# Value sums of the second attention: from VectorE reductions to accumulating transposes on TensorE

## The reference

```
q = q.reshape(Tq, Bq * H, HD).transpose(1, 0, 2)      # k and v alike
attn = jnp.einsum('nqd,nkd->nqk', q, k) * scale
attn = jax.nn.softmax(attn, axis=-1)                  # over 8 keys
out = jnp.einsum('nqk,nkd->nqd', attn, v)             # the value sums
out = out @ out_w.T + out_b
x = x + attention(xn) + moe(xn)
```

## Time and profile before

| | |
|---|---|
| median of 3 runs | 407.57 us |
| profiled execution, its own time | 408.92 us |
| its span, first to last instruction | 407.1 us |
| mean granted clock of TensorE | 0.937 |
| PE / DVE / POOL / ACT busy | 79% / 85% / 58% / 46% |
| DVE's reductions of prod_pv (L1358) | 32 of 1195 ns, 38.2 us |
| POOL's prod_pv (L783) | 32 of 2212 ns, 69.6 us |

### The profile page before, as it was taken

The page is one execution under the profiler, slowest core; times in us unless marked ns, Lnnn a source line. Parts: engine busy times, 40 slices in busy tenths (PEclk is TensorE's granted clock), DMA queues, the critical chain, the costliest instruction groups (busy, mean ns, idle before and its releaser), DMA issues.

```text
span 407.1 us, 5016 instructions
## 1 busy us (share of the span) xinstructions
PE 323.2 (79%) x1455; PEld 237.0 (58%) x1455; DVE 344.1 (85%) x831; ACT 188.4 (46%) x501; POOL 235.4 (58%) x149
## 2 busy tenths in 40 slices
PE   0267696898898875805129999999999999999995
PEld 0136475777787765704016666666666666666662
DVE  3774997987887964599999899999999999999791
ACT  0535556778678656702122262624426262442521
POOL 9151573553644721095065959778695986867450
PEclk9986998999999999775758999999999999999999
DMA  7620000100100102220000000000000000000000
GB/s 184 209 77 1 2 0 1 54 37 17 52 22 32 53 27 96 91 52 0 1 0 1 2 0 27 2 26 0 0 28 1 26 2 26 1 2 26 0 26 27
DMA packets 13247, 12.49 MB, mean 31 GB/s; under 512 B 1548, under 2 KB 9924, under 8 KB 13220
## 3 DMA queue, kind: packets, MB, share of 16 engines
q1 hardware_dynamic: 10944, 10.10, 7.7%
q0 software_dynamic: 736, 0.95, 1.2%
q10 hardware_dynamic: 1540, 1.12, 0.9%
HBM read 5.88 MB, written 2.10 MB: 20 GB/s over the span
## 4 chain that ended last, share of the span: by engine, by line
PE 54%; DVE 19%; ACT 11%; issue 7%; POOL 6%; DMA 1%; ACTq 1%; POOLq 0%; DVEq 0%
PE Q L833 18%; PE VK L833 16%; PE T L833 9%; PE ND L833 6%; PE T L829 4%; ACT xn L546 4%; POOL prod_qk L773 3%; POOL prod_pv L783 2%; PE Q L829 2%; ACT qkv L503 1%; DMA headmask<-in_c_headsel 1%; ACT Q L585 1%; DVE chosen L1411 1%; DVE bst L1086 1%; DVE scr L1341 1%
## 5 line engine op out<-in xcount | busy, mean ns | idle before, releaser
L783 POOL TENSOR_TENSOR prod_pv<-prob,qkv 128x1024 f32<-128x1024 f32 x32 | 69.6, 2212 | 45.0 <-DVE att L1358 24.3
L686 ACT ACTIVATE sg<-Q 128x512 f32<-128x512 f32 x72 | 43.2, 599 | 97.7 <-PE Q L833 95.0
L773 POOL TENSOR_TENSOR prod_qk<-qkv 128x1024 f32<-128x1024 f32 x32 | 75.9, 2397 | 16.7 <-DVE scr L1341 16.7
L833 PE MATMUL VK<-hid,w 128*128 128x512 f32 x144 | 74.5, 599 | 0.0
L833 PE MATMUL Q<-xT_hi,w_hi 128*128 128x512 f32 x72 | 52.3, 726 | 0.7 <-ACT combT L672 0.7
L1441 DVE TENSOR_TENSOR sgc<-ND,sg 128x512 f32<-128x512 f32 x64 | 43.6, 681 | 6.7 <-PE ND L833 4.7
L1454 DVE TENSOR_TENSOR hid<-T,sgc 128x512 f32<-128x512 f32 x64 | 43.5, 679 | 0.3
L833 PE MATMUL T<-xT_hi,w_hi 128*128 128x512 f32 x72 | 28.9, 401 | 17.0 <-DVE hid L1454 17.0
L833 PE MATMUL Q<-bias,ones 128*128 128x384 f32 (+1 forms) x64 | 32.8, 512 | 9.4 <-ACT qkv L503 5.8
L1341 DVE TENSOR_REDUCE scr<-prod_qk 128x128 f32<-128x1024 f32 x32 | 38.4, 1205 | 0.0
L1358 DVE TENSOR_REDUCE att<-prod_pv 128x128 f32<-128x1024 f32 x32 | 38.2, 1195 | 0.0
(11 more groups left out here) (190 smaller groups left out, 796.9 us busy)
## 6 DMA issues: line engine op xcount, KB each, us to landing
xT_hi<-xTs_hi SPq DMA_DIRECT2D x8, 256.0 KB, 2.3
xT_lo<-xTs_lo SPq DMA_DIRECT2D x8, 256.0 KB, 2.3
out_x<-fin SPq DMA_DIRECT2D x8, 256.0 KB, 2.3
x<-in_x SPq DMA_DIRECT2D x2, 256.0 KB, 4.7
wraw<-in_w1T SPq DMA_DIRECT2D x1, 512.0 KB, 10.8
w<-in_w2T SPq DMA_DIRECT2D x1, 512.0 KB, 4.6
wraw<-in_w3T ACTq DMA_DIRECT2D x1, 512.0 KB, 3.1
sel<-in_c_sel POOLq DMA_DIRECT2D x4, 128.0 KB, 2.8
```

The source lines that it names most:

```text
L686: act.activation(sg[:, side(half, s), :], QB[side(half, s)][:, :], ACT.Silu).then_inc(sg_ready, 1)
L773: pool.tensor_tensor(prod_qk[:, t % 2], bc(qkv2[:, TH * half + t, j, 0:D], 1, NB), qkv2[:, :, j, D:2 * D], ALU.mult).then_inc(qk_prod, 1)
L783: pool.tensor_tensor(prod_pv[:, t % 2].rearrange("p (h e) b -> p b h e", e=HD), bc(prob[:, t], 3, HD), qkv2[:, :, j, 2 * D:QKV].rearrange( ...
L833: return pe.matmul(o, lhsT, rhs, start=start, stop=stop)
```

## The change

PE now adds over the keys. A transpose on PE is a matmul with the identity, and its result may be added to what the PSUM bank holds. For each query 8 transposes, one per key, go to the same 128 columns of Q2: the sum over the keys comes out already transposed, as attT is. `values(n, t)` on PE issues them behind `down` in steps 5, 6, 7 and 8, for t = 0 to 3. DVE's reduction and the tile att are gone. The division moves ahead of the products: POOL multiplies prob by the reciprocals in place, and only then by the values. The key now stands outside in prod_pv, which has four buffers instead of two. The reciprocal moves on DVE from step 3 to step 2, right behind the sum. The wait for `fin_ready` (Q2 free of the last slot's output) moves on PE from step 8 to step 5.

The core of the diff:

```diff
-        prod_pv = sb("prod_pv", [P, 2, D, NB])
+        prod_pv01 = sb("prod_pv01", [P, 2, NB, D])
...
-        att = sb("att", [P, TH, D])
...
+        prod_pv23 = sb("prod_pv23", [P, 2, NB, D])
+        prod_pv = lambda t: (prod_pv01, prod_pv23)[t // 2][:, t % 2]
...
-                        evac(attT[:, :, :], tiles(Q2), (attT_ps, n + 1), [], attT_ready)
+                        evac(attT[:, :, :], tiles(Q2), (pv_T, TH * n + TH), [], attT_ready)
...
             def products_pv(n, j):
 
-                pool.wait_ge(p_ready, n + 1)
+                pool.wait_ge(p_sum, 2 * n + 2)
+                pool.tensor_tensor(prob[:, :, :, :], prob[:, :, :, :], bc(psum_p[:, 1], 2, NB), ALU.mult)\
+                    .then_inc(p_normal, 1)
+                pool.wait_ge(p_normal, n + 1)
                 for t in range(TH):
                     u = TH * n + t
-                    after(pool, pv_red, u - 1)
+                    after(pool, pv_T, u - TH + 1)
                     settle(pool)
                     pool.tensor_tensor(
-                        prod_pv[:, t % 2].rearrange("p (h e) b -> p b h e", e=HD),
+                        prod_pv(t).rearrange("p b (h e) -> p b h e", e=HD),
...
-            def normalise(n):
-
-                pool.wait_ge(p_sum, 2 * n + 2)
-                pool.wait_ge(pv_red, TH * n + TH)
...
-            def attention_transposes(n):
-                pe.wait_ge(att_ready, n + 1)
-
-                after(pe, fin_ready, n)
-                transposes(Q2, lambda t: att[:, t, :], signal=attT_ps)
+            def values(n, t):
+
+                pe.wait_ge(pv_prod, TH * n + t + 1)
+                if t == 0:
+                    after(pe, fin_ready, n)
+                for b in range(NB):
+                    m = pe.matmul(Q2[:, t * D:(t + 1) * D], prod_pv(t)[:, b, :], ident[:, :], is_transpose=True,
+                                  start=t == 0 and b == 0, stop=t == TH - 1 and b == NB - 1)
+                m.then_inc(pv_T, 1)
...
-                    if s == NS - 1:
+                    if s >= NS - TH:
                         if at(n, 0):
                             pe.wait_ge(combT_ready, 2)
-                        attention_transposes(n)
+                        values(n, s - (NS - TH))
...
-            def values(n, t):
-                u = TH * n + t
-                dve.wait_ge(pv_prod, u + 1)
-                if t == 0:
-                    after(dve, attT_ps, n)
-                V.tensor_reduce(att[:, t], prod_pv[:, t % 2], AX_X, ALU.add)\
-                    .then_inc(pv_red, 1)
...
                         sum_of_p(n)
+                        over_sum(n)
...
-                    if s == 3:
-                        over_sum(n)
-                    if 3 <= s < 3 + TH:
-                        values(n, s - 3)
```

More of the change, by code:

```diff
@@ L335, in build @@
         pv_prod = sem("pv_prod")
-        pv_red = sem("pv_red")
+        pv_T = sem("pv_T")
+        p_normal = sem("p_normal")
         p_sum = sem("p_sum")
-        att_ready = sem("att_ready")
-        attT_ps = sem("attT_ps")
         attT_ready = sem("attT_ready")
@@ L798, in _ @@
             pool.wait_ge(comb2_ready, 2)
-            def normalise(n):
-                pool.wait_ge(p_sum, 2 * n + 2)
-                pool.wait_ge(pv_red, TH * n + TH)
-                heads = lambda a: a[:, :, :].rearrange("p t (h e) -> p t h e", e=HD)
-                pool.tensor_tensor(heads(att), heads(att), bc(psum_p[:, 1], 3, HD), ALU.mult)\
-                    .then_inc(att_ready, 1)
             def slot(n, j, half):
@@ L819, in slot @@
                 next_qk(3)
-                normalise(n)
             slots(pool, slot)
@@ L1351, in less_max @@
                     .then_inc(s_sub, 1)
-            def values(n, t):
-                u = TH * n + t
-                dve.wait_ge(pv_prod, u + 1)
-                if t == 0:
-                    after(dve, attT_ps, n)
-                V.tensor_reduce(att[:, t], prod_pv[:, t % 2], AX_X, ALU.add)\
-                    .then_inc(pv_red, 1)
             def sum_of_p(n):
                 dve.wait_ge(p_ready, n + 1)
-                after(dve, att_ready, n)
+                after(dve, p_normal, n)
                 V.tensor_reduce(psum_p[:, 0], prob[:, :, :, :].rearrange("p t b h -> p t h b"), AX_X, ALU.add)\
```

## The result

The changed kernel takes 431.09 us, median of 4 runs (430.17 to 433.71), against 407.78 us of the kernel before beside it. The ratio is 1.0557, with a 95% interval of 1.0516 to 1.0597. The prediction said 430.7 us, +23.1; the medians are 23.3 apart. The profiled execution took 433.71 us, the slowest of the four. Its span of 431.9 us is 24.8 longer than that of before, but 1.28 of that lies ahead of the first slot's T matmuls (212.77 against 211.49 us), where nothing was changed. So I count in slots.

A forecast was written before the change was run, and what follows sets the result against it. PE's own work was taken to bound the kernel: 24.6 us of added transposes less 1.5 us of waits, +23.1 on a median of 407.57, gives 430.7 us; 8-in-10 range 427.5 to 436.

The forecast's parts named there:

- What bounds the kernel: Second-layer slots are the sum of PE's own work, 23.74 of 23.78 us; DVE's waits cost 1.50 us in six slots.
- A transpose at 0.11 us: PE's groups of eight behind `down`: 0.88 us each, 3.08 us more per slot, 24.6 us over eight slots.
- The wait for `att` gone, 1.5 us: PE's transposes no longer wait for POOL's normalisation of att: 1.50 us back, if nothing takes its place.
- The reciprocal ahead of `sgc` and `hid`: DVE, step 2: these come 0.54 us later, which fits with 0.3 to spare; without cover, up to 2.4 us in all.
- The cover of the products: POOL's four products, 2.2 us each, are ready before PE wants them: first 2.8 us in hand, last 5.9.
- A: Rival: each PE transpose waits for the last, adding to the same columns, 0.273 us each; 472 us; chance 4%.
- D: Rival: each transpose's weight load on PE hides behind the matmul before, 0.055 us each; 418 us; chance 3%.
- B: Rival: PE's clock falls in the four steps with transposes, some 40 us more in all; 471 us; chance 2%.
- E: Rival: DVE was the bound, so taking its reductions shortens slots, by at most 30 us; 378 us; chance 2%.
- C: Rival: POOL becomes the bound, at 4.4 us a product 28.3 us per slot against PE's 26.9; 441 us; chance 5%.

The follow-up runs named there:

- kernel with one key and the sum first: Changed kernel with only the first key's transpose per query, and DVE's sum over prob and reciprocal ahead of the second prod_qk reduction: 406.66 us, ratio 0.9956.
- with one key: Changed kernel with only the first key's transpose for each query, the other seven keys' products left out of the sums: 413.94 us, ratio 1.0118.

## Why the prediction was right, step by step

**What bounds the kernel: right.** The slot as a sum of PE's pieces, 23.74 of 23.78 us, held against a DVE that was 97% busy. The transposes alone on the old kernel give the changed kernel's time.

**A transpose at 0.11 us: right.** 0.87 us for eight, and 0.110 from the pair of kernels that differ by 224 of them (and by DVE's order in step 2). Neither a wait for the add (0.273) nor a hidden load (0.055) shows; the row of `VK<-v_ext,kf` was the proper one to go by. The Trainium skill ("TensorE: Matmul & The Clock Gate", Part 4: PE-mode transpose) gives about 275 ns for one in one kernel's context. The trace agrees with it as a duration, 272 ns:

```profile
L1019 PE MATMUL Q<-ident,prod_pv 128*128 128x128 f32 x256 | 33.1, 272 | 0.0
```

As a price in a row of transposes it would be 2.5 times too high, as the chain shows.

**The wait for `att` gone, 1.5 us: right in the size, with a reason that was not needed.** Slots went from 23.78 and 24.1 to 26.83 alike. I put this down to the division that moves; the transposes added alone lose the wait too, with the division where it was. The kernel with one key and the sum first shows 1.9 us on the median, four buffers alone 1.9 as well. I had not seen that this gain was to be had without the transposes.

**The reciprocal ahead of `sgc` and `hid`: right that it costs nothing, with the wrong cover.** I gave it 0.3 us to spare. In the changed kernel `hid` of step 2 ends at 327.46 and PE's T matmul of step 4 starts at 328.23, 0.77 later, since the subtraction before it takes 0.69 instead of 1.12 us: the longer slot keeps POOL's prod_qk away from it.

**The cover of the products: right in the result, mis-sized in the margin.** For PE's own wait I was right: the first product is ready at 327.74 + 1.98 = 329.72, 2.9 us before PE's first group at 332.64, where I had 2.8 in hand (the division takes 1.27 us, where I had 1.09). But I let POOL decide only from its summed work, at some 4 us a product. The runs show a loop instead, which dividing first makes: POOL's work of a slot plus 6.2 us on DVE, 24.83 us against PE's 26.83. The true margin is, by an estimate from these two, 2.0 us a slot or 0.5 us a product, so that products of 2.5 us would have begun to cost. For 4.4 us a product I gave 441 us; at 3.96 us the kernel takes 468.7. With the 2.2 to 2.4 us that I took, the loop would have come to 25.7 to 26.5 us, still under PE's slot, and with the old layout it measures 25.35; the contiguous layout, at 1.98 us, was not needed for the sum. That the loop does not show in the changed kernel is luck: it hides behind the 3 us that the transposes add to PE's slot, and where they were taken out, with one key, it cost 7 us (413.94 against 406.66).

**Rivals.** A and D fall by the group of eight, B by the clock of 1.00, E by the transposes added alone. C named the right neighbour with too small a price.

## What to carry to other kernels

Where the chain of waits over one period is the sum of one engine's pieces, moving work onto that engine costs its full price, however busy the engine is that it is taken from: a DVE that was 97% busy gave back 1.9 us at most, and two more buffers gave the same. Price an instruction by the distance that several of them make in the chain, never by its duration. And before judging how much slack an engine has, follow the loop through it (its work plus the way back over the other engines), for its idle time need not be free: here 7.8 us idle a slot held 2.0 us of slack. A step that is moved ahead of others, as the division is here, can close such a loop.

## What the runs showed of the hardware

DVE's subtraction has both inputs in SBUF, and in every case looked at it did not get through while POOL multiplied. With POOL idle it takes 0.69 us. In the kernel before it took 1.12, ending 0.54 us after POOL's prod_qk did (307.48 against 302.16 + 4.78 = 306.94); with one key 1.78, ending 0.55 after it; and in the first slot of the kernel before 2.69, ending 0.55 after it (208.15 + 2.69 = 210.84 against 205.64 + 4.65 = 210.29). The rows of slot 4 of the kernel before:

```profile
306.36 1.12 DVE L1350 TENSOR_TENSOR scr<-scr,smax 128x512 f32<-128x512 f32 x1
```

```profile
302.16 4.78 POOL L773 TENSOR_TENSOR prod_qk<-qkv 128x1024 f32<-128x1024 f32 x2
```

`sgc` and `hid`, which read one input from PSUM, take 0.68 us beside a busy POOL too. The Trainium skill ("GPSIMD Engine Reference", Key points) says that GpSimd shares its SBUF interfaces with VectorE, with contention for instructions with two SBUF inputs. The trace agrees, and gives the size here: the subtraction waited for the end of POOL's work, with 0.6, 1.2 or 2.1 us of it left. Each time POOL was at the last of several products in a row; whether the subtraction would get through between two is not shown.

POOL's product with the key outside, contiguous, takes 1.98 us, against 2.21 with the key innermost (2.23 where the division also comes first); its division of prob, with the reciprocal repeated in the middle dimension, takes 1.27, against 1.09 for that of att.
